# One-hots for two tables at a time, one piece of gram per tile, and layer 3 in four column groups in a DLRM tower

## What is computed

```python
e = jnp.stack([tbl_0[ids[:, 0]], ..., tbl_25[ids[:, 25]]], axis=1)
all_vecs = jnp.concatenate([dense_proj[:, None, :], e], axis=1)
interactions = jnp.einsum('bnd,bmd->bnm', all_vecs, all_vecs)
interact_flat = interactions[:, rows, cols]          # n < m
z = jnp.concatenate([dense_proj, interact_flat], axis=1)
h = jnp.concatenate([z, r_dense_proj], axis=1)
h = jnp.maximum(h @ W_top1 + b_top1, 0.0)            # 607 -> 512
h = jnp.maximum(h @ W_top2 + b_top2, 0.0)            # 512 -> 256
y = h @ W_top3                                       # 256 -> 1
```

## Time and profile before

| | us |
|---|---|
| median of 3 runs (370.31 to 371.07) | 370.9 |
| the profiled execution | 370.56 |
| its span | 368.6 |
| PE busy | 338.4 (92%) |
| DVE busy | 241.6 (66%) |
| POOL busy | 245.3 (67%) |
| ACT busy | 140.9 (38%) |
| a pair of tiles on PE in the loop: start of layer 1 in tile 8 (218.48) to that in tile 10 (260.15) | 41.7 |
| a gather: from one start on POOL to the next (198.07, 199.32) | 1.25 |

### The profile page before, as it was taken

One profiled execution on the slowest core, in us unless ns is written; L12 is line 12 of the kernel. 1 busy time (PEld: TensorE's weight loads), 2 busy tenths in 40 slices (PEclk: granted clock), 3 DMA queues, 4 the chain that ended last, 5 costly groups with the idle time before them and its releaser, 6 DMA issues.

```text
span 368.6 us, 14267 instructions
## 1 busy us (share of the span) xinstructions
PE 338.4 (92%) x6096; PEld 309.5 (84%) x6096; DVE 241.6 (66%) x702; ACT 140.9 (38%) x232; POOL 245.3 (67%) x260
## 2 busy tenths in 40 slices
PE   0686689999999999999999999999999999999797
PEld 0585589999899898989899998989999998998675
DVE  4999999998565856578565974677664884601300
ACT  2246432535143541344343441444442450447132
POOL 5777777777777777777777777777767777760000
PEclk9989999999999999999999999999999999999999
DMA  6999944332244212611243111521244112220000
GB/s 192 284 245 245 290 140 124 79 106 54 58 152 123 59 50 67 205 56 52 55 145 125 50 51 50 188 83 50 52 140 129 50 50 55 73 57 4 18 2 0
DMA packets 16567, 36.90 MB, mean 100 GB/s; under 512 B 5462, under 2 KB 8542, under 8 KB 16544
## 3 DMA queue, kind: packets, MB, share of 16 engines
q1 hardware_dynamic: 8335, 19.77, 18.0%
q0 software_dynamic: 8192, 16.79, 17.6%
q10 hardware_dynamic: 16, 0.01, 0.0%
HBM read 36.54 MB, written 0.01 MB: 99 GB/s over the span
## 4 chain that ended last, share of the span: by engine, by line
PE 85%; DVE 7%; issue 3%; DMA 3%; POOL 2%; ACT 0%; DVEq 0%
PE hid L387 14%; PE gram L413 13%; PE look_ps L341 8%; PE vec_act L314 7%; PE look_ps L343 7%; PE look_odd L341 7%; PE look_odd L343 7%; PE hid L394 7%; DVE onehot L557 5%; PE hid L341 4%; PE hid L343 4%; DMA vecs<-tbl,ids_sb 2%; DVE look_lo L565 2%; POOL vecs L297 2%; PE small L356 1%
## 5 line engine op out<-in xcount | busy, mean ns | idle before, releaser
L297 POOL DMA_INDIRECT vecs<-tbl,ids_sb x256 | 245.1, 957 | 85.1 <-issue 75.9
L557 DVE TENSOR_SCALAR onehot<-step_ids,row_no 125x256 fp32r<-125x256 int32 x640 | 199.0, 381 | 74.6 <-PE look_odd L343 35.0
L532 ACT COPY vecs_T<-vec_act 128x512 f32<-128x512 f32 x64 | 46.3, 732 | 102.2 <-PE vec_act L314 102.2
L341 PE MATMUL look_odd<-onehot,look_hi 125*128 125x256 f32 x256 | 67.3, 300 | 4.6 <-DVE look_lo L565 4.6
L341 PE MATMUL look_ps<-onehot,look_hi 125*128 125x256 f32 x256 | 67.8, 301 | 2.3 <-DVE look_lo L565 2.3
L343 PE MATMUL look_ps<-onehot,look_lo 125*128 125x256 f32 x256 | 63.7, 284 | 0.0
L343 PE MATMUL look_odd<-onehot,look_lo 125*128 125x256 f32 x256 | 62.9, 283 | 0.0
L413 PE MATMUL gram<-vecs_T 128*27 128x26 f32 x4096 | 52.8, 192 | 5.9 <-issue 3.3
L413 PEld LDWEIGHTS gram<-vecs_T 128*27 128x27 f32 x4096 | 44.1, 104 | 15.0 <-issue 9.1
L341 PEld LDWEIGHTS look_odd<-onehot,look_hi 125*128 125x128 f32 x256 | 48.8, 191 | 5.5 <-DVE look_lo L565 5.2
L341 PEld LDWEIGHTS look_ps<-onehot,look_hi 125*128 125x128 f32 x256 | 49.2, 192 | 3.2 <-DVE look_lo L565 2.7
(11 more groups left out here) (70 smaller groups left out, 282.2 us busy)
## 6 DMA issues: line engine op xcount, KB each, us to landing
step_ids<-look_ids SPq DMA_DIRECT2D x15, 640.0 KB, 4.5
raw<-tbl SPq DMA_DIRECT2D x10, 448.0 KB
vecs<-tbl,ids_sb POOLq DMA_INDIRECT x256
dense_new<-dense SPq DMA_DIRECT2D x8, 128.0 KB
dense_T<-dense SPq DMA_DIRECT2D x8, 128.0 KB, 2.9
raw<-tbl SPq DMA_DIRECT2D x10, 52.0 KB
step_ids<-look_ids SPq DMA_DIRECT2D x1, 512.0 KB
w_sb<-w SPq DMA_DIRECT2D x1, 512.0 KB
```

Source lines behind the costliest of these rows:

```text
L297: nc.gpsimd.indirect_dma_start(out=vecs[j][:, k, :], out_offset=None, in_=tables[k], in_offset=bass.IndirectOffsetOnAxis(ap=ids_sb[:, t, k ...
L341: nc.tensor.matmul(bank, look_hi[:, f, ch, :], onehot[:, i % SLOTS, c, :], start=ch == 0, stop=False)
L532: return engine_copy(vecs_T[j][:, :, lo:lo + GROUP], bank[:, :, :].rearrange("d v b -> d b v"))
L557: last = nc.vector.tensor_scalar(onehot[:, i % SLOTS, c, :], step_ids[a][0:LOOK_K, f - a * LOOKUPS // 2, :], row_no[0:LOOK_K, ch:ch + 1], ...
```

## The change

- One DVE instruction compares 512 ids, those of two tables, with the row numbers of a chunk. A unit is now two chunks of a duo, four units to a duo; the slots keep their size and number. PE's lookups alternate between the two tables of the duo. The ids come as tables 0 to 3 and 4 to 9 of a pair instead of the two halves.
- In the start (the first pair) PE takes a duo in two passes, first all chunks of its first table, then of its second (`look_up_first`); a slot is given back in the second pass. ACT's and DVE's order there is written out anew, and the first turn groups stand before the third duo.
- `gram` is one piece (`gram_all`), after unit 8, with unit 9 behind it (and behind layer 3 in odd tiles). `gram_half0` and POOL's wait for it are gone.
- Layer 3 uses weights padded to 32 columns and four column groups, each for 64 of the 256 samples; `y` comes out as four rows of 64 for a pair.
- After the loop: gram of tile 14, pairs_out of tile 13, half of layer 1, all four turn groups of tile 15, the other half of layer 1, gram of tile 15.

```diff
-UNIT_CH = LOOK_CH // 2
+UNIT_CH = LOOK_CH // 4
...
-        onehot = sb("onehot", [LOOK_K, SLOTS, UNIT_CH, PAIR], F32R)
+        onehot = sb("onehot", [LOOK_K, SLOTS, UNIT_CH, 2 * PAIR], F32R)
...
-                        if k == HALF_GATHERS and t >= 2:
-                            pool.wait_ge(gram_half0, t - 1)
-                            pool.sem_inc(gather_begun, 1)
...
+                def look_up_first(duo):
+
+                    wait_for_bank(0, duo)
+                    for v in range(2):
+                        pe.wait_ge(table_split, 2 * duo + v + 1)
+                        for part in range(DUO_UNITS):
+                            n = duo * DUO_UNITS + part
+                            if v == 0:
+                                pe.wait_ge(onehot_made, n + 1)
+                            for c in range(UNIT_CH):
+                                last = look_chunk(duo, v, part, c, n % SLOTS)
+                            if v == 1:
+                                last.then_inc(onehot_used, 1)
...
+                def layer3_parts(bank):
+
+                    for c in range(H2 // P):
+                        for g in range(Y_PARTS):
+                            last = nc.tensor.matmul(bank[g * QUAD:(g + 1) * QUAD, :], w3_sb[:, c, :],
+                                                    h2_T[:, c, g * PAIR // Y_PARTS:(g + 1) * PAIR // Y_PARTS],
+                                                    start=c == 0, stop=c == H2 // P - 1)
+                    return last
...
-                    gram_first(t, j, pair)
...
-                    unit(9)
-                    gram_second(j)
+                    gram_all(t, j, pair)
                     if mlp and j == 1:
                         layer3(pair - 1)
+                    unit(9)
...
-                tile(last - 1, 0, pairs - 1, look=False)
+                gram_all(last - 1, 0, pairs - 1)
+                pairs_out(last - 2, 0, pairs - 1)
+                layer1(pairs - 2, 0, look=False)
+                turn_half(last, 1, pairs - 1, 0)
+                turn_half(last, 1, pairs - 1, 1)
                 layer1(pairs - 2, 1)
-                gram_first(last, 1, pairs - 1)
-                gram_second(1)
+                gram_all(last, 1, pairs - 1)
...
                         last = nc.vector.tensor_scalar(
-                            onehot[:, i % SLOTS, c, :], step_ids[a][0:LOOK_K, f - a * LOOKUPS // 2, :],
+                            onehot[:, i % SLOTS, c, :],
+                            pair_ids[0:LOOK_K, 2 * duo:2 * duo + 2, :].rearrange("p f b -> p (f b)"),
                             row_no[0:LOOK_K, ch:ch + 1], None, ALU.is_equal)
```

226 lines of the change are left out of this document (125 added, 101 removed).

## The result

The changed kernel takes 388.67 us (median of 4 runs, 387.57 to 390.51), the kernel before in the same comparison 370.99 (370.31 to 371.51). The ratio is 1.0483, 95% interval 1.0433 to 1.0532. The profiled execution took 387.57 us; its span is 385.7 us against 368.6. So the sign was right and the size was not: the span grew by 17.1 us where the sum had +7.0, and the median lies above the range of 370 to 384.

A forecast was written before the change was run, and what follows sets the result against it. PE was taken as the bound (85% of the chain), nearly without a gap after a DVE-bound start. Terms summed to +7.0 us on a span of 368.6, giving 375.6, execution 377.6, forecast 378 us, range 370 to 384.

The forecast's parts named there:

- start, DVE and PE: First lookups, two tables at a time: over at 48.7 us instead of 46.5, +2.2 us, between 0 and +4.
- gathers late: POOL's gathers: 40.0 us for a pair that takes PE about 41.7, none late after the start, so no cost.
- gram: one entry and exit less: Gram in one piece: one entry and exit less, 0.2 us in each of 14 tiles, -2.8 us.
- odd grams: Gram in odd tiles, mostly undisturbed by gathers at 2.5 us: -1.0 us, with +5 as the other bound.
- fetch in tiles 0 to 3: Instruction fetch stops PE inside the one-piece grams there: +0.2 us in tile 0, +1.1 in each other, +3.5.
- late turn, at pairs_out: PE waits about 0.75 us in pairs_out for DVE's turn of the last gram, seven times: +5.3 us, between 0 and +7.
- layer 3 in the tiles: Layer 3 in four column groups running together: 0.35 us instead of 0.87, six times, -3.0 us.
- low clock: Slow lookups (0.21 us, not 0.12) after long PE idle, costed only inside the start: +1.1 us per 12 slow ones.
- end: After the loop: tile 14's fetch stall, waits for ACT and a further layer2 block, less layer 3's gain: +2.8 us.
- POOL is near, yet no gather is late after the start.: Gathers come every 1.25 us, 40.0 for a pair taking PE 41.7, so no cost was given for waits.
- POOL's idle time must fall into the first three parts: Odd tiles: POOL's 1.5 to 2 us of idle per pair falls in gram's first three parts, leaving it 2.5 us.
- slower rival: Odd grams disturbed by gathers (+5 more) and PE always slow in the start (+1.8): 385 us; chance 0.12.

The follow-up runs named there:

- after_narrow: Also called the narrow version: changed kernel with each 512-column one-hot made by two instructions of 256 columns, all else as it is; 385.59 us, ratio 1.0383.
- before_wide: Kernel before with only 512-column one-hots for two tables and the start in pairs of tables; 381.98 us, ratio 1.0263.
- after_narrow_two: Changed kernel with 256-column one-hots and gram of tiles 0 to 13 in two pieces; 377.08 us, ratio 1.0165.
- after_unit9: Changed kernel with unit 9 ahead of gram instead of behind it; median 390.57 us, executions from 384.32 to 392.30, ratio 1.0516.
- before_gram1: Kernel before with gram in one piece behind unit 9, tile 14's too, and without POOL's wait for gram_half0; 380.53 us, ratio 1.0153.
- before_l3: Kernel before with layer 3 in four column groups alone; 368.67 us, ratio 0.9916.
- after_old_end: Changed kernel with the order of the kernel before behind the loop; 384.83 us, ratio 1.0358.

## Why the prediction was right in sign and wrong in size

By the steps of its sum, against the changed kernel's span:

| step | forecast us | measured us |
|---|---|---|
| start, DVE and PE | +2.2 | -2.6 |
| gathers late | 0 | +8.5 |
| gram: one entry and exit less | -2.8 | not to be seen apart |
| odd grams | -1.0 | +3.1 |
| fetch in tiles 0 to 3 | +3.5 | +3.9 |
| late turn, at pairs_out | +5.3 | +2.9 |
| layer 3 in the tiles | -3.0 | -3.1 |
| low clock | 0 outside the start | +3.4 |
| end | +2.8 | +1.3 |

The measured column: the end of the first lookups (43.9 and 46.5); the waits of the profile after less those of before (fetch: 1.09, 1.66, 1.23 and 1.18 less the 1.26 of the earlier trace rows); the odd grams of tiles 5 to 13, 18.5 us in five groups against 15.4 in the ten pieces of before; layer 3's 0.51 times six; low clock 5.1 less 1.7; the end from the traces behind the loop (37.8 less 36.5). With -2.8 for the gram's entries, taken as forecast, the column sums to 14.6 of the 17.1 us; what the other 2.5 us are is open.

**The step that failed: "POOL is near, yet no gather is late after the start."** I costed the 512-column one-hot on VectorE and for PE, and never asked what it does to the engine beside it. So the sum has gathers' waits at 0 where 8.5 us came, its largest miss. POOL was given its old rate, one gather per 1.25 us, and 40.0 us of a 41.7 us pair. The trace showed how little room that is; the wide one-hots raise POOL's busy time in a pair of tiles to 32.5 us (30.7 before), and by 46 us in the start four gathers fewer have begun than in the narrow version, six fewer than in the kernel before. after_narrow takes the width away and the waits go; before_wide brings the wide one-hots without the one-piece gram and they come; after_narrow_two has the order by pairs without the width, and no wait. This much is shown. What it is worth is less than the waits: narrow one-hots in the same order have no wait and gain 3 to 4 us.

When a gather becomes long the traces show (after_narrow above): when a compare or a split of VectorE is under way as it begins, and by about what is left of it. Why is not shown. The Trainium skill (SBUF — State Buffer, SBUF: two separate sides) names a mechanism: VectorE and GpSimd share a pair of SBUF ports, a VectorE instruction in a two-port mode holds it whole until it ends, and GpSimd can't write the descriptors of its DMAs meanwhile. Here the long gathers agree with that: they last 0.94 us and most of the rest of the instruction beside them (0.29 more for 0.42 left, 0.59 for 0.71). The narrow one-hots, 0.32 us each and twice as many, leave the gathers at 0.94 us in the median because little of one is left when a gather begins. Which instructions hold the ports was not tested: the split with two inputs lengthens gathers, copies and transposes don't. By the rule, the question of the neighbour would have been asked before the run.

**The start was mis-sized the other way.** The term rested on 0.59 us for a 512-column one-hot, near the upper of two bounds (0.32 and 0.64). It takes 0.41 (six in 2.47 us at 21.97). The row for the line to 1024 columns was the split's, another operation with two inputs. The low pace of PE came for the first 16 lookups (0.21 us apart, to 14.53) and not behind the later idle times of the start. The term also summed 1.92, 0.48 and 0.2 us to 2.65 instead of 2.60, and the late turn's 3.85 is 3.81 by its parts; neither matters.

**The late turn was right in place and mechanism, and too large.** The same 0.41: VectorE's unit and turn are over sooner, and 0.51 us are left of 0.75. With narrow one-hots the waits are 6.1 us, more than forecast; after_unit9 shows that the order of unit 9 makes them, and that as much idle time comes out at the branch in their place (3.0 us in six turns); its execution times are too far apart to tell a gain.

**Instruction fetch: right in place nearly to the record, and in size (+3.9 for +3.5).** Four stops in tiles 0 to 3 and one in tile 14, at 209, 236, 235, 222 and 195 records (206, 227, 233, 223, 190 forecast), none in the loop. The sentence of the Trainium skill (Runtime: NRT & Kernel Launch, Instruction fetch mechanics) that crossing a block is "mostly hidden" does not hold in these traces for a gram of 256 short instructions: before_gram1's six grams that are executed once all stop, for 1.3 to 2.5 us. Nearly everywhere else it does (before_l3 stops once in layer 2, for 0.62 us). Tile 15 is the miss: forecast after 136 records, it did not come. Tile 14 had two stops instead, one ahead of its first record and one after 195; by the instruction queue the fetch had its lead for tile 15 (363.52, gram from 364.88); that the stops in tile 14 gave it is my reading, not shown by a run.

**Odd grams: the step "POOL's idle time must fall into the first three parts" failed.** Longer gathers left POOL no idle time in a pair (from 170 to 215 us it never pauses for more than the 0.3 us between two gathers; the narrow version pauses three times, up to 1.77 us), so gathers ran through the odd grams too: 3.77 us in tiles 5 and 7, and down to 3.48 in tile 13. The prediction had this as the bound of +5 and as half of its slower rival, with a chance of 0.12; the other half, a slow start, did not happen. The right rival stood there for want of the right reason.

**Low clock.** The forecast knew one row at half clock behind an idle time of 3.40 us and used it only inside the start. Every new idle time of one to three us later on was a candidate too. It took 5.1 us of PE time instead of 1.7 in the profiled execution, some 10 in after_narrow, and makes the times of these kernels spread.

**Layer 3** was right: 0.36 us for a forecast 0.35. But the kernel before would have kept almost none of it in the loop (before_l3): there the long layer 3 hid the branch.

**The end** cost +1.3 us and not +2.8, with other parts: tile 14's stops 3.5 us instead of 2.2, ACT waits of 0.57 and 0.50, no stop in tile 15 (2.13 before) and no further block in layer 2. That tile 15's stop goes was not forecast; against after_old_end, whose stop there is 0.70, the new order costs 3.4.
